# Recurrence output products of a batch: one block of matmuls, or five parts spread over the next two tiles

## The chip, the cores and the metric

The kernel runs on one core of one Trainium2 chip. The metric is the device time of one execution in microseconds (us). The core has five engines with instruction queues of their own: TensorE (PE, matmuls and their weight loads), VectorE (DVE), ScalarE (ACT), GpSimd (POOL) and SyncE (SP, which issues the DMAs). They meet at semaphores.

## What is computed

The reference is one pre-norm layer over x with 4096 rows of 256: an attention block and a small feed-forward block, each added to its input. The attention has 16 heads of 16 channels and two ways to an output, which a gate mixes.

```python
qkv = (x @ Wqkv_w + Wqkv_b).reshape(Bb, Ll, 3, Hh, dd)
attn = jax.nn.softmax(scores + causal_mask, axis=-1)
y_softmax = jnp.einsum('bhij,bhjd->bhid', attn, v)
def step(state, inp):
    q_t, k_t, v_t = inp
    hebbian = v_t[..., :, None] * k_t[..., None, :]
    state = retention * state + Gamma * hebbian
    y_t = jnp.einsum('bhij,bhj->bhi', W_static + state, q_t)
    return (state, y_t)
y = alpha * y_softmax + (1.0 - alpha) * y_stp
```

The second way is a linear recurrence over all 4096 time steps with a 16 x 16 state for each head, whose output at every step is the state (and a static matrix) times the query.

## The kernel before, in words

There are three stages: normalisation and projections (up to about 230 us), attention and recurrence side by side (up to about 1950 us), and a last stage with gate, output projection and feed-forward. The change lies in the middle one.

*Softmax attention.* Four heads make a group, and there are four groups. Queries stand in 8 chunks of 512, taken in the order of `ORDER`, keys in tiles of 128. A group has 144 tiles (`TILES`): one tile is 128 keys against one chunk of queries, for four heads. In a tile TensorE makes four score products `S` (`scores`, L1150, keys by queries, each into a bank of its own), ScalarE takes the exponential of each into `probs` (L1279), and one tile later TensorE makes the values product `V` (`values`, L1166: eight matmul instructions for the four heads, each in a quarter of the columns, into the bank `O_BANK`). The shift in the exponential has to be known before, so the maxima of later chunks are worked out beside this: product `M` (`max_scores`, L1110, queries by keys), of which two side by side go into two banks, and VectorE reduces both with one instruction (L1329). A tile has four `M`, so two maxima. Scores and maximum products use one half of TensorE's rows each (heads stand on two sides), so two that stand next to each other in the order and use different sides run side by side.

*Recurrence.* It runs over 64 units for a group, 16 batches of four (`BATCH`). SyncE loads `v_exp` for each unit (L930), GpSimd multiplies with the keys (L1044), ScalarE scales (L1288), GpSimd sums blocks of four steps (L1054 to L1065), VectorE scans (L1364), and GpSimd weighs the states with the queries (`weigh`, L1077, four instructions, which count the semaphore `weighed`). Then TensorE contracts them: `burst` (L1199) makes static products (L1211), lag products (L1213) and the state products of the four units (L1219), all accumulated in one bank, 128 columns of it. ScalarE evacuates it (`burst_evac`, L1308, to `stp_sb`), and SyncE stores it (L982).

*The order.* Each engine walks the same list of steps, made by `group_steps` (L172), and takes what is its own. In a tile, `TILE_ORDER` (L84) gives the order: S an attention score product, M a maximum product, V values of the tile before and then what `contract` adds, U the evacuations that are due and the recurrence's other steps. `recurrence_steps` (L127) says in which tile they are due: batch B has its period of 9 tiles (8 in the last group); its scan is in tile 9B + 1, its burst after the values of tile 9B + 6, and the evacuation at U of the following tile, behind that tile's first score. `lag` steps and the transposes of shifts and outputs (`turn`, at a tile's end) stand in the same list.

*The banks.* PSUM has eight: three (`S_BANKS`) go round in rotation (`next_bank`) among scores, bursts, lags and turns, four are for maxima, one for the values. `emptied_before` (L258) gives each user of a bank what it has to wait for: the exponential, evacuation or turn that emptied it.

Of the kernel before, what the change touches and what calls it, by code (L numbers as in the profile page):

```python
# [63 lines left out]
STEP4 = 4  # L64
BLOCKS = CH // STEP4
LAGS = STEP4 - 1
# [14 lines left out]
S_BANKS = 3  # L81
M_BANKS = 4
O_BANK = S_BANKS + M_BANKS
TILE_ORDER = "SUMMSSMMSV"  # L84
RING = 2 * BATCH
PAIR = CH // 2
UNITS_PER_CHUNK = 7
# [84 lines left out]
def group_steps(last):  # L172


    steps, turns, pending, evacuations = [], [], [], []
    todo = [(0,) + x for x in ITEMS[AHEAD:]] + ([] if last else [(1,) + x for x in ITEMS[:AHEAD]])
    used = 0
    recurrence = recurrence_steps(last)

    def next_bank():  # L180
        nonlocal used
        used += 1
        return (used - 1) % S_BANKS

    def maximum():
        d, s, n = todo.pop(0)
        steps.append(("max", d, s, n))
        if n == MAXES[s] - 1:
            steps.append(("fold", d, s))
            turns.append([SHIFT_LEAD, "shift_turn", "shift_split", d, s])  # L190

    def turn():
        if turns and turns[0][0] > 0:
            turns[0][0] -= 1
        elif turns:
            _, into, out_of, d, s = turns.pop(0)
            bank = next_bank()
            steps.extend([(into, d, s, bank), (out_of, d, s, bank)])

    def values():  # L200
        s, kt = pending.pop(0)
        steps.append(("values", 0, s, kt))
        if kt == KEY_TILES[s] - 1:
            steps.append(("out_evac", 0, s))
            turns.append([OUT_LEAD, "out_turn", "out_norm", 0, s])

    def recurrent(t, kinds):
        for step in recurrence.get(t, ()):
            if step[0] in kinds:
                steps.append(step)  # L210

    def contract(t):
        for step in recurrence.get(t, ()):
            if step[0] in ("burst", "lag"):
                bank = next_bank()
                steps.append(step + (bank,))
                evacuations.append((step[0] + "_evac",) + step[1:] + (bank,))

    for s in range(NCH):
        for kt in range(KEY_TILES[s]):  # L220
            t = TILE_AT[s] + kt
            for d, names in ((0, LATER), (1, [] if last else EARLY)):
                for name in names:
                    n = t - LOADS[name][2] - d * TILES
                    if 0 <= n < transfers(name):
                        steps.append(("load", d, name, n))
            h = 0
            for kind in TILE_ORDER:
                if kind == "S":
                    steps.append(("scores", 0, s, kt, h, next_bank()))  # L230
                    h += 1
                elif kind == "M" and todo:
                    maximum()
                elif kind == "V":
                    if pending:
                        values()
                    contract(t)
                elif kind == "U":
                    steps.extend(evacuations)
                    evacuations.clear()  # L240
                    recurrent(t, ("kq_load", "v_load", "scan", "scale"))
            turn()
            pending.append((s, kt))
    assert not todo and max(recurrence) < TILES
    values()
    steps.extend(evacuations)
    while turns:
        turns[0][0] = 0
        turn()
    return steps  # L250
# [7 lines left out]
def emptied_before(steps, tail):  # L258


    found, before = {}, dict(tail)
    counts = {"exp": 0, "turn": 0, "burst": 0, "lag": 0}
    for x in steps:
        if x[0] == "scores":
            kind, bank, fills, empties = "exp", x[5], True, True
        elif x[0] in ("shift_turn", "out_turn"):
            kind, bank, fills, empties = "turn", x[3], True, True
        elif x[0] in ("burst", "burst_evac"):
            kind, bank, fills, empties = "burst", x[3], x[0] == "burst", x[0] == "burst_evac"
        elif x[0] in ("lag", "lag_evac"):  # L270
            kind, bank, fills, empties = "lag", x[4], x[0] == "lag", x[0] == "lag_evac"
        else:
            continue
        if fills:
            found[x[:{"exp": 5, "lag": 4}.get(kind, 3)]] = before.get(bank)
        if empties:
            before[bank] = (kind, counts[kind])
            counts[kind] += 1
    return found, {bank: (kind, n - counts[kind]) for bank, (kind, n) in before.items()}
# [12 lines left out]
def preln_attention_ffn_kernel(nc, x, wqkv, bqkv, out_w, out_b, w_static, lam, gamma, gate_w1,  # L292
                               gate_b1, gate_w2, gate_b2, ffn_wt, ffn_b, out):
    ctx = ExitStack()
    with ctx:
# [563 lines left out]
        with att:  # L859
# [22 lines left out]
            with nc.Block() as block:  # L882
# [226 lines left out]
                def _(pe):  # L1109
# [86 lines left out]
                            at += width  # L1196
                        mm.then_inc(lag_ready, 1)

                    def burst(g, B, bank):  # L1199
                        b, q = B // SWEEP_BATCHES, B % SWEEP_BATCHES  # L1200
                        half = b % HALF

                        def rows(e):
                            return PS[e * VW:(e + 1) * VW, bank, 0:BLOCKS]

                        if q == 0:
                            pe.wait_ge(lag_summed, g * (2 * N_SWEEPS) + 2 * b + 2)
                        pe.wait_ge(weighed, g * UNITS + BATCH * B + BATCH + 2 * BATCH)
                        now = q_rows[:, b % 2, 1:1 + CH].rearrange("p (c e) -> p e c", e=STEP4)
                        for e in range(STEP4):  # L1210
                            pe.matmul(rows(e), static_j[:, half, q * VW:(q + 1) * VW], now[:, e], start=True, stop=False)  # L1211
                        for e in range(LAGS):
                            pe.matmul(rows(e), ident[:, q * VW:(q + 1) * VW], lags[:, b % 2, e * BLOCKS:(e + 1) * BLOCKS],  # L1213
                                      start=False, stop=False)
                        for k in range(BATCH):
                            own = state[:, B % 2, k]
                            for e in range(STEP4):
                                first = 1 + e if e < LAGS else 0
                                mm = pe.matmul(rows(e), sum_e[:, half, q * BATCH + k, e, :],  # L1219
                                               own[:, 1 + e:1 + e + STEP4 * (BLOCKS - 1) + 1:STEP4],  # L1220
                                               start=False, stop=(k == BATCH - 1))
                        mm.then_inc(burst_done, 1)

                    def walk(group, steps, emptied, turns_before):
                        for step in steps:
                            kind, g, s = step[0], group + step[1], step[2]
                            if kind == "max":
                                max_scores(g, s, step[3])
                            elif kind == "scores":
                                wait_emptied(group, emptied[step[:5]], turns_before)  # L1230
                                scores(g, s, step[3], step[4], step[5])
                            elif kind == "values":
                                values(g, s, step[3])
                            elif kind == "burst":
                                wait_emptied(group, emptied[step[:3]], turns_before)
                                burst(g, s, step[3])
                            elif kind == "lag":
                                if emptied[step[:4]]:
                                    wait_emptied(group, emptied[step[:4]], turns_before)
                                lag(g, s, step[3], step[4])  # L1240
                            elif kind == "shift_turn":

                                pe.wait_ge(folded, g * NCH + s + 1)
                                if emptied[step[:3]]:
                                    wait_emptied(group, emptied[step[:3]], turns_before)
                                pe.transpose(PS[0:GH * TPC, step[3], 0:P], neg_max[:, s % 2, :], ident[:, :])\
                                    .then_inc(shift_turned, 1)
                            elif kind == "out_turn":

                                pe.wait_ge(out_evacuated, g * NCH + s + 2)  # L1250
                                wait_emptied(group, emptied[step[:3]], turns_before)
                                for j in range(TPC):
                                    mm = pe.transpose(PS[:, step[3], j * P:(j + 1) * P], o_t[:, s % 2, j * P:(j + 1) * P],
                                                      ident[:, :])
                                mm.then_inc(out_turned, 1)
# [499 lines left out]
```

## Time and profile before

| what | us |
|---|---|
| time, median of 3 runs | 2127.93 |
| lowest and highest of them | 2119.26, 2133.13 |
| profiled execution, its own time | 2120.3 |
| its span, first to last instruction | 2118.6 |

The span leaves 1.7 us of the execution's own time outside. The rows further down are of this execution. "Idle" in brackets is the time that an engine stood still just before the instruction, with the one that released it behind the arrow. Rows of a timeline are merged: x2 means two instructions, and the time beside the start is what they cover together.

### The profile page before, as it was taken

The numbers are of one execution on the slowest core, as the hardware profiler recorded it, in microseconds if no ns is written. First come the engines' busy times: TensorE is split into PE (matmuls) and PEld (weight loads), VectorE is DVE, ScalarE is ACT, GpSimd is POOL, SyncE is SP. The second block draws the span as 40 slices with busy tenths as digits, with TensorE's granted clock in tenths as the row PEclk, the third lists the DMA queues.
The fourth block names the chain that finished last, engine by engine and source line by source line (L and its number), as shares of the span: only waits on it lengthen the run. The fifth ranks groups of instructions, "written<-read, shape, count | busy, mean of one in ns | idle before, by whom it ended". The sixth has DMA issues, their size and how long they took to land. (4 is left out here: it accounts for less than half of the span.)

```text
span 2118.6 us, 47123 instructions
## 1 busy us (share of the span) xinstructions
PE 1800.1 (85%) x15280; PEld 718.8 (34%) x15280; DVE 1558.5 (74%) x1712; ACT 1368.7 (65%) x2853; POOL 1153.0 (54%) x1130
## 2 busy tenths in 40 slices
PE   5995589999999899999989999999899998986743
PEld 3552133333334333333343323333433233322632
DVE  5334988888788778887878888878888788601767
ACT  2441067777776777777767777777677777875221
POOL 3102246565666566666666666666567757630535
PEclk9996589999999999999999999999999999998865
DMA  4778041232122412321224124112242121102601
GB/s 127 194 192 198 12 89 59 67 78 64 50 67 66 95 57 69 79 66 50 66 63 99 56 65 94 55 47 79 59 107 67 46 75 45 51 8 57 190 0 79
DMA packets 144582, 163.60 MB, mean 77 GB/s; under 512 B 63440, under 2 KB 91088, under 8 KB 144336
## 3 DMA queue, kind: packets, MB, share of 16 engines
q1 hardware_dynamic: 141952, 158.74, 27.9%
q8 instruction: 131, 2.15, 0.4%
q10 hardware_dynamic: 2384, 1.77, 0.3%
q14 instruction: 115, 0.94, 0.2%
HBM read 122.00 MB, written 38.01 MB: 76 GB/s over the span
## 5 line engine op out<-in xcount | busy, mean ns | idle before, releaser
L1329 DVE TENSOR_REDUCE pmax<-PS 128x2 f32<-128x1024 f32 (+3 forms) x1152 | 1252.5, 1131 | 268.1 <-PE PS L1126 218.2
L1279 ACT ACTIVATE probs<-PS 128x512 f32<-128x512 f32 (+3 forms) x2304 | 1149.5, 566 | 441.9 <-PE PS L1160 336.5
L1160 PE MATMUL PS<-Q_st,K_st 50*128 50x512 f16 (+3 forms) x1408 | 419.0, 360 | 65.9 <-ACT stp_sb L1308 24.7
L1126 PE MATMUL PS<-K_st,Q_st 48*128 48x512 f16 (+3 forms) x1408 | 349.2, 360 | 23.4 <-DVE pmax L1329 22.1
L1181 PE MATMUL PS<-probs,V_g 128*17 128x512 f32 (+3 forms) x2816 | 339.2, 554 | 0.0
L1044 POOL TENSOR_TENSOR v_exp<-v_exp,k_rows 128x512 f32<-128x512 f32 x256 | 321.1, 1287 | 16.7 <-DMA v_exp<-qkv_t 13.7
L1160 PE MATMUL PS<-Q_st,K_first 50*128 50x512 f16 (+3 forms) x896 | 281.6, 382 | 38.8 <-ACT stp_sb L1308 15.2
L1126 PE MATMUL PS<-K_first,Q_st 48*128 48x512 f16 (+2 forms) x896 | 240.6, 413 | 54.3 <-DVE pmax L1329 40.8
L1077 POOL TENSOR_TENSOR state<-ends,q_rows 128x516 f32<-128x516 f32 x256 | 276.1, 1111 | 0.0
L1072 POOL COPY carry<-ends 128x4 f32<-128x4 f32 x64 | 12.1, 189 | 457.1 <-DVE ends L1364 457.1
L1160 PEld LDWEIGHTS PS<-Q_st,K_st 50*128 50x128 f16 x1408 | 113.6, 93 | 418.4 <-ACT probs L1279 296.2
L1054 POOL TENSOR_TENSOR pairs<-pairs,v_exp 128x512 f32<-128x512 f32 x128 | 165.7, 1295 | 135.2 <-ACT pairs L1288 135.2
L1181 PE MATMUL PS<-probs,V_first 128*17 128x512 f32 (+3 forms) x1792 | 230.2, 586 | 0.0
L1160 PEld LDWEIGHTS PS<-Q_st,K_first 50*128 50x128 f16 x896 | 73.3, 94 | 289.1 <-ACT probs L1279 203.3
L1219 PE MATMUL PS<-state,sum_e 128*32 128x128 f32 x2048 | 142.9, 408 | 0.0
L1288 ACT ACTIVATE pairs<-v_exp,decay 128x256 f32<-128x256 f32 x256 | 132.5, 519 | 0.3
L1135 PE MATMUL PS<-mask_kq_sides,ident_sides 64*128 64x128 bf16 x1024 | 124.7, 215 | 0.0
L1126 PEld LDWEIGHTS PS<-K_st,Q_st 48*128 48x128 f16 x1408 | 84.4, 93 | 75.4 <-DVE pmax L1329 68.5
L1135 PE MATMUL PS<-mask_qk_sides,ident_sides 64*128 64x128 bf16 x1024 | 104.9, 222 | 0.0
L1219 PEld LDWEIGHTS PS<-state,sum_e 128*32 128x32 f32 x2048 | 90.7, 123 | 20.0
L1364 DVE TENSOR_TENSOR_SCAN ends<-decay_x,sums 128x516 f32<-128x516 f32 x64 | 79.3, 1240 | 22.4 <-POOL sums L1065 22.4
L621 PE MATMUL PS<-xn_t,wqkv_sb 128*128 128x512 f32 x192 | 94.2, 652 | 1.8 <-ACT xn_t L678 1.8
(163 smaller groups left out, 1569.8 us busy)
## 6 DMA issues: line engine op xcount, KB each, us to landing
v_exp<-qkv_t SPq DMA_DIRECT2D x256, 256.0 KB
qkv_t<-proj SPq DMA_DIRECT2D x24, 512.0 KB, 3.7
qk_parts<-parts SPq DMA_DIRECT2D x16, 512.0 KB, 5.3
Q_st<-qk_parts SPq DMA_DIRECT2D x192, 32.0 KB, 3.4
v_rows<-vaug SPq DMA_DIRECT2D x32, 136.0 KB, 6.1
xin<-x SPq DMA_DIRECT2D x8, 512.0 KB, 6.0
k_rows<-qkv_t SPq DMA_DIRECT2D x16, 256.0 KB, 4.7
q_rows<-qkv_t SPq DMA_DIRECT2D x16, 256.0 KB, 6.8
```

The costliest lines, as they stand in the source:

```text
L621: mm = pe.matmul(PS[:, 2 + u % 4, :], w, xn_t[:, par, c, :], start=(c == 0), stop=(c == HALF - 1))
L1044: pool.tensor_tensor(v_exp[:, n % RING], v_exp[:, n % RING], k_rows[:, b % 2], ALU.mult)\
L1054: pool.tensor_tensor(pairs[:, B % 2, k:k + 2], pairs[:, B % 2, k:k + 2], v_exp[:, slot:slot + 2, 1:CH:2], ALU.add).then_inc(pair_made, 1)
L1077: pool.tensor_tensor(state[:, B % 2, k].rearrange("p (c e) -> p c e", e=STEP4), ends[:, B % 2, k].unsqueeze(2).broadcast_to([P, BLOCKS + 1 ...
L1126: mm = pe.matmul(PS[:, bank, 0:width], Q_st[rows, c, pair, j * P:(j + 1) * P], keys[rows, pair, blk * CH:blk * CH + width], start=True, st ...
L1135: mm = pe.matmul(bank, ident_sides[rows, half, :], mask[rows, half, :], start=False, stop=(half == 1))
L1160: mm = pe.matmul(PS[:, bank, 0:CH - r * P], keys[rows, pair, kt * P:(kt + 1) * P], Q_st[rows, c, pair, r * P:CH], start=True, stop=(kt < T ...
L1181: mm = pe.matmul(PS[h * VW:h * VW + VN, O_BANK, r * P:CH], v[:, kt, h * VN:(h + 1) * VN], probs[:, tile % P_SLOTS, h, 0:CH - r * P], start ...
L1219: mm = pe.matmul(rows(e), sum_e[:, half, q * BATCH + k, e, :], own[:, 1 + e:1 + e + STEP4 * (BLOCKS - 1) + 1:STEP4], start=False, stop=(k ...
L1279: act.activation(probs[:, tile % P_SLOTS, h, 0:CH - r * P], PS[:, step[5], 0:CH - r * P], ACT.Exp, scale=SCORE_SCALE).then_inc(exp_done, 1)
L1288: act.activation(pairs[:, B % 2, s % BATCH, :], v_exp[:, s % RING, 0:CH:2], ACT.Identity, scale=decay[:, 0, col:col + 1]).then_inc(u_scale ...
L1329: dve.tensor_reduce(pmax[:, s % 2, pair * TPC + j:GH * TPC:PAIRS * TPC, blk], PS[:, bank:bank + SIDES, 0:width], AX.X, ALU.max).then_inc(m ...
```

## The change

`TILE_ORDER` gets three places `R` in a tile: after the first pair of maximum products, after the second and third score, and after the second pair of maximum products. A burst is no longer issued after the values of its tile. There its bank is only taken (`held`) and five parts are queued (`BURST_PARTS`): part 0 has the static and lag products, parts 1 to 4 the state products of one unit each. Each `R` issues one part if there is one: three in the next tile, two in the one after. While the bank is held, `next_bank` skips it, so that two banks go round. The evacuation is due at the U after the last part, and the bank is given back there, before the second score of that tile is given its bank. The wait for `weighed` is made for each unit instead of once for the batch. With no part queued, the order of a tile is as before.

```diff
--- before.py
+++ after.py
@@ -81,7 +81,8 @@
 S_BANKS = 3
 M_BANKS = 4
 O_BANK = S_BANKS + M_BANKS
-TILE_ORDER = "SUMMSSMMSV"
+TILE_ORDER = "SUMMRSSRMMRSV"
+BURST_PARTS = 1 + BATCH
 RING = 2 * BATCH
 PAIR = CH // 2
 UNITS_PER_CHUNK = 7
@@ -175,11 +176,14 @@
     steps, turns, pending, evacuations = [], [], [], []
     todo = [(0,) + x for x in ITEMS[AHEAD:]] + ([] if last else [(1,) + x for x in ITEMS[:AHEAD]])
     used = 0
+    held, parts = [], []
     recurrence = recurrence_steps(last)
 
     def next_bank():
         nonlocal used
         used += 1
+        while (used - 1) % S_BANKS in held:
+            used += 1
         return (used - 1) % S_BANKS
 
     def maximum():
@@ -211,10 +215,20 @@
 
     def contract(t):
         for step in recurrence.get(t, ()):
-            if step[0] in ("burst", "lag"):
+            if step[0] == "lag":
                 bank = next_bank()
                 steps.append(step + (bank,))
                 evacuations.append((step[0] + "_evac",) + step[1:] + (bank,))
+            elif step[0] == "burst":
+                held.append(next_bank())
+                parts.extend([step + (held[0], part) for part in range(BURST_PARTS)])
+
+    def burst_part():
+        if parts:
+            step = parts.pop(0)
+            steps.append(step)
+            if not parts:
+                evacuations.append(("burst_evac",) + step[1:4])
 
     for s in range(NCH):
         for kt in range(KEY_TILES[s]):
@@ -235,8 +249,12 @@
                     if pending:
                         values()
                     contract(t)
+                elif kind == "R":
+                    burst_part()
                 elif kind == "U":
                     steps.extend(evacuations)
+                    if "burst_evac" in [x[0] for x in evacuations]:
+                        held.clear()
                     evacuations.clear()
                     recurrent(t, ("kq_load", "v_load", "scan", "scale"))
             turn()
@@ -266,7 +284,7 @@
         elif x[0] in ("shift_turn", "out_turn"):
             kind, bank, fills, empties = "turn", x[3], True, True
         elif x[0] in ("burst", "burst_evac"):
-            kind, bank, fills, empties = "burst", x[3], x[0] == "burst", x[0] == "burst_evac"
+            kind, bank, fills, empties = "burst", x[3], x[0] == "burst" and x[4] == 0, x[0] == "burst_evac"
         elif x[0] in ("lag", "lag_evac"):
             kind, bank, fills, empties = "lag", x[4], x[0] == "lag", x[0] == "lag_evac"
         else:
@@ -1196,30 +1214,33 @@
                             at += width
                         mm.then_inc(lag_ready, 1)
 
-                    def burst(g, B, bank):
+                    def burst(g, B, bank, part):
                         b, q = B // SWEEP_BATCHES, B % SWEEP_BATCHES
                         half = b % HALF
 
                         def rows(e):
                             return PS[e * VW:(e + 1) * VW, bank, 0:BLOCKS]
 
+                        if part > 0:
+                            k = part - 1
+
+                            pe.wait_ge(weighed, g * UNITS + BATCH * B + k + 1 + 2 * BATCH)
+                            own = state[:, B % 2, k]
+                            for e in range(STEP4):
+                                mm = pe.matmul(rows(e), sum_e[:, half, q * BATCH + k, e, :],
+                                               own[:, 1 + e:1 + e + STEP4 * (BLOCKS - 1) + 1:STEP4],
+                                               start=False, stop=(k == BATCH - 1))
+                            if k == BATCH - 1:
+                                mm.then_inc(burst_done, 1)
+                            return
                         if q == 0:
                             pe.wait_ge(lag_summed, g * (2 * N_SWEEPS) + 2 * b + 2)
-                        pe.wait_ge(weighed, g * UNITS + BATCH * B + BATCH + 2 * BATCH)
                         now = q_rows[:, b % 2, 1:1 + CH].rearrange("p (c e) -> p e c", e=STEP4)
                         for e in range(STEP4):
                             pe.matmul(rows(e), static_j[:, half, q * VW:(q + 1) * VW], now[:, e], start=True, stop=False)
                         for e in range(LAGS):
                             pe.matmul(rows(e), ident[:, q * VW:(q + 1) * VW], lags[:, b % 2, e * BLOCKS:(e + 1) * BLOCKS],
                                       start=False, stop=False)
-                        for k in range(BATCH):
-                            own = state[:, B % 2, k]
-                            for e in range(STEP4):
-                                first = 1 + e if e < LAGS else 0
-                                mm = pe.matmul(rows(e), sum_e[:, half, q * BATCH + k, e, :],
-                                               own[:, 1 + e:1 + e + STEP4 * (BLOCKS - 1) + 1:STEP4],
-                                               start=False, stop=(k == BATCH - 1))
-                        mm.then_inc(burst_done, 1)
 
                     def walk(group, steps, emptied, turns_before):
                         for step in steps:
@@ -1232,8 +1253,9 @@
                             elif kind == "values":
                                 values(g, s, step[3])
                             elif kind == "burst":
-                                wait_emptied(group, emptied[step[:3]], turns_before)
-                                burst(g, s, step[3])
+                                if step[4] == 0:
+                                    wait_emptied(group, emptied[step[:3]], turns_before)
+                                burst(g, s, step[3], step[4])
                             elif kind == "lag":
                                 if emptied[step[:4]]:
                                     wait_emptied(group, emptied[step[:4]], turns_before)
```

## Rows read from the trace of the kernel before

**Rows 1.** Page: the span, busy time by engine (share of the span, instructions)
```profile
span 2118.6 us, 47123 instructions
...
PE 1800.1 (85%) x15280; PEld 718.8 (34%) x15280; DVE 1558.5 (74%) x1712; ACT 1368.7 (65%) x2853; POOL 1153.0 (54%) x1130
```

**Rows 2.** Page, costliest groups: busy us, mean ns | idle us before, what ended it
```profile
L1329 DVE TENSOR_REDUCE pmax<-PS 128x2 f32<-128x1024 f32 (+3 forms) x1152 | 1252.5, 1131 | 268.1 <-PE PS L1126 218.2
```

**Rows 3.** Timeline of VectorE around a burst: start us, us, operation [idle before <-releaser]
```profile
911.74 7.12 DVE L1329 TENSOR_REDUCE pmax<-PS 128x2 f32<-128x1024 f32 x6 [0.55 <-PE PS L1126]
921.37 2.26 DVE L1329 TENSOR_REDUCE pmax<-PS 128x2 f32<-128x1024 f32 x2 [2.52 <-PE PS L1126]
924.27 4.74 DVE L1329 TENSOR_REDUCE pmax<-PS 128x2 f32<-128x1024 f32 x4 [0.64 <-PE PS L1126]
```

**Rows 4.** Timeline of TensorE, from an ordinary tile through a burst to tile 8
```profile
915.85 0.39 PE L1160 MATMUL PS<-Q_st,K_st 50*128 50x512 f16 x1
915.85 0.60 PE L1126 MATMUL PS<-K_st,Q_st 48*128 48x512 f16 x2
916.08 0.59 PE L1160 MATMUL PS<-Q_st,K_st 50*128 50x512 f16 x2
916.53 0.39 PE L1126 MATMUL PS<-K_st,Q_st 48*128 48x512 f16 x2
916.93 0.39 PE L1160 MATMUL PS<-Q_st,K_st 50*128 50x512 f16 x1
917.24 1.05 PE L1181 MATMUL PS<-probs,V_g 128*17 128x512 f32 x8
918.11 0.64 PE L1211 MATMUL PS<-q_rows,static_j 128*32 128x128 f32 x8
...
918.79 2.01 PE L1219 MATMUL PS<-state,sum_e 128*32 128x128 f32 x31
920.73 0.39 PE L1160 MATMUL PS<-Q_st,K_st 50*128 50x512 f16 x1
...
921.97 0.39 PE L1160 MATMUL PS<-Q_st,K_st 50*128 50x512 f16 x1 [0.64 <-ACT stp_sb L1308]
...
922.65 1.05 PE L1181 MATMUL PS<-probs,V_g 128*17 128x512 f32 x8
923.63 0.39 PE L1160 MATMUL PS<-Q_st,K_st 50*128 50x512 f16 x1
```

**Rows 5.** Source line L1219, matmuls: duration ns min/median/max
```profile
L1219 PE MATMUL PS<-state,sum_e x2048: 385/408/429, 292.5 to 1902.2; 128*32 128x128 f32 x187
```

**Rows 6.** Timeline of ScalarE, exponentials and the evacuation of the burst
```profile
921.15 0.60 ACT L1279 ACTIVATE probs<-PS 128x512 f32<-128x512 f32 x1 [2.81 <-PE PS L1160]
921.65 0.27 ACT L1308 ACTIVATE stp_sb<-PS 128x128 f32<-128x128 f32 x1
...
916.27 0.60 ACT L1279 ACTIVATE probs<-PS 128x512 f32<-128x512 f32 x1 [0.31 <-PE PS L1160]
```

**Rows 7.** Timelines of VectorE, then TensorE, around the scan of another batch
```profile
483.84 1.22 DVE L1364 TENSOR_TENSOR_SCAN ends<-decay_x,sums 128x516 f32<-128x516 f32 x1
484.98 6.37 DVE L1329 TENSOR_REDUCE pmax<-PS 128x2 f32<-128x1024 f32 x6
...
484.69 1.05 PE L1181 MATMUL PS<-probs,V_g 128*17 128x512 f32 x8
...
487.36 0.39 PE L1126 MATMUL PS<-K_st,Q_st 48*128 48x512 f16 x2 [0.53 <-DVE pmax L1329]
...
487.90 1.05 PE L1181 MATMUL PS<-probs,V_g 128*17 128x512 f32 x8
```

**Rows 8.** Timelines of SyncE (queue), then GpSimd, after the burst of rows 4
```profile
923.53 3.31 SPq L930 DMA_DIRECT2D v_exp<-qkv_t  x4
...
930.46 4.31 POOL L1077 TENSOR_TENSOR state<-ends,q_rows 128x516 f32<-128x516 f32 x4
...
945.62 4.95 POOL L1044 TENSOR_TENSOR v_exp<-v_exp,k_rows 128x512 f32<-128x512 f32 x4
```

## The prediction

> **What bounds the kernel now.** I read the page first. TensorE has the most busy time, 85% of the span, VectorE 74% [rows 1]; but the busy time of overlapping matmuls is no proof of a bound, so the question is who waits in the attention stage. The costliest group is VectorE's maxima (L1329): 268 us of idle time stand before them, 218 of it ended by a score matmul of TensorE [rows 2]. The VectorE timeline around one burst shows where that idle time lies: maxima run without a gap from 911.74 for 7.12 us, then come 2.52 us of idle time, two maxima, and 0.64 us more [rows 3]. That is 3.16 us for a burst, and 64 bursts make 202 of the 268 us. The TensorE timeline of the same place [rows 4] shows what VectorE waits for. I call the tile whose end holds the burst tile 6 (as in the first period of nine) and those after it 7, 8, 9.
>
> An ordinary tile takes 2.375 us: VectorE does six maxima, three tiles, in 7.12 us [rows 3]. TensorE isn't full in it. Scores S0 and the first maximum product start together at 915.85, one on each half of the rows; the next two scores start 0.23 and 0.44 later; the second pair of maximum products 0.68 after the start; S3 at 1.08; values at 1.39, and they take 0.98 until the next score (922.65 to 923.63) [rows 4]. S3 reuses S0's bank and starts when S0's exponential is out: that begins 0.42 after S0 and lasts 0.60 [rows 6]. Without waits the eight products, two side by side, want four steps of 0.22, so TensorE needs 0.88 + 0.98 = 1.87 us and has 0.5 us of waiting in a tile, which an inserted part could use.
>
> **What a burst costs.** Values begin at 917.24, the burst at 918.11, the next score at 920.73 [rows 4]. Values to score takes 0.98 otherwise, so the burst adds 3.49 - 0.98 = 2.50 us. In tile 7, S2 wants the burst's bank and is held until 921.97, 1.24 us after S0, by the evacuation, which stands behind S0's exponential on ScalarE [rows 4, 6]. That tile takes 2.90 (920.73 to 923.63), 0.52 over an ordinary one. Together 3.02 us.
>
> **The change part by part.** The matmuls stay the same in number and shape. Part 0 has static and lag products: 918.11 to the first of the 31 state products at 918.79, 0.68 us. The state products start within 2.01 us, less the 0.41 of the last one [rows 4, 5]: the last starts at 920.39. A record of 0.41 against the 0.17 by which a 512-column score's record (0.39) exceeds the 0.22 step leaves 0.23 of streaming, so the array is free at 920.62, and the four state parts take 1.84 / 4 = 0.46 each.
>
> *Changing between the kinds.* Score and maximum products use half the rows and all columns, burst and values products all rows and a quarter of the columns. From rows 4: S3 to values takes 0.31 where one product streams for about 0.22, so entering costs 0.10. The array is free at 920.62 and the score starts at 920.73, so leaving costs 0.10 (0.11 without rounding). Values to burst takes 0.87 against 0.98 to a score: no such gap between two products of one kind. Now the burst stands behind values and is entered free; after the change each of five parts is entered from scores or maxima and left to them. By my reading the rule in the Trainium skill, TensorEngine Tiling (Array Packing), Key Properties, that a change of the tiling mode drains TensorE, is this effect; the trace agrees, with 0.10 and 0.11 us here; without it the sum would be the first rival's.
>
> *Tile 7* is then, from S0: S0 beside the first maximum product 0; the second alone 0.22 (S1, its neighbour now, stands behind the part); part 0 at 0.53, ends 1.21; S1 beside S2 1.31; part 1 at 1.62 to 2.08; maxima 2.18; part 2 at 2.49 to 2.95; S3 3.05; values 3.36; tile 8 at 4.35. *Tile 8*: second product 0.22; part 3 at 0.53 to 0.99; S1, S2 1.09; part 4 at 1.40 to 1.86; maxima 1.96; S3 2.18; values 2.49; tile 9 at 3.48. Together 7.83, where burst, tile 7's and tile 8's ordinary lengths take 2.50 + 2 x 2.375 = 7.25 now. So +0.58 us a burst, x 64 = +37 us. The 0.5 us of waiting in each tile is used, but ten changes at about 0.1 and two lost pairings at 0.22 eat more.
>
> *Two score banks.* A bank is free 0.42 + 0.60 + 0.05 = 1.07 after its score (915.85 to 916.93 is such a pair) [rows 4, 6]. In the times above S2 comes 1.31 and 1.09 after S0, and S3 1.74 and 1.09 after S1: all just past it. So nothing, at most 0.1 a tile. VectorE's maxima, at most 1.23 each, have time inside 4.35 and 3.48. Behind the waiting score stand maxima products, but those pairs of banks are then free anyway.
>
> *The evacuation* moves to tile 9. Counting the rotation through (burst bank X, then X+1, X+2 alternately until the next step U), S2 of tile 9 takes X again, with the evacuation behind S0's exponential as now: the same 0.52 us, moved by two tiles. Nothing is gained.
>
> *The scan.* The scan of the next batch now goes alone into a full VectorE in tile 10: 1.22 us, maxima follow without a gap, and TensorE's second pair waits 0.53 for them; values come 3.21 after the last instead of 2.375 [rows 7], a delay of 0.84. With the change tile 10 follows the 2.90 us tile directly. A pair is ready 0.64 after its tile's start (920.73 to 921.37 [rows 3, 4]). In tile 9 the second pair, issued behind the held S2 at 1.33, is ready at 1.97 and reduced by 3.20; the first pair of tile 10 is ready at 2.90 + 0.64 = 3.54. So 0.34 of the scan lies in a gap. The scan ends at 4.42 and two queued maxima, 2.26 together as at 921.37 [rows 3], at 6.68; tile 11 starts at 2.90 + 2.38 = 5.28 and can issue its second pair at about 6.77, 1.5 after its start, where now it is 1.69 (484.69 + 0.98 to 487.36 [rows 7]). So 0.2 comes back: 48 bursts of the first three groups, -10 us (between 0 and -0.34 x 48 = -16). In the last group the period is 8, and scan and evacuation share a tile: the last maximum of tile 8 ends at 0.13, the scan at 1.37, two queued maxima at 3.63, where the next pair is ready at 3.54; so 0.8 comes back, 15 times: -12 us (between 0 and -13).
>
> *Turns.* About 25 transposes fall at the end of tile 7 or 8 and use one of two banks; VectorE frees it before S1, which stands behind a part. +2 us (0 to +5).
>
> *Queues.* SP issues the burst's store and, right behind, the four v_exp loads of a later batch; they go at 923.53 and are wanted at 945.62 [rows 8]. Two tiles later, about 6 us, leaves 16. GpSimd needs the burst only two batches on. So this costs nothing; with less than 6 us between the two, GpSimd, VectorE's scan and then the bursts would be late by what is missing.
>
> **Sum.** 37 - 10 - 12 + 2 = +17 us on the profiled execution's own 2120.3 (the span of 2118.6 and 1.7 around it, which stay), so 2137. That execution is 7.6 us under the median 2127.9 of the runs; on it I forecast 2145, +0.8%. A measurement of this kernel can tell about 1% from no change.
>
> **Rivals.**
> A. *Changes are free* (weights of the next kind load while the last stream runs). Then tile 7 is 0.43 + 0.68 + 0.22 + 0.46 + 0.22 + 0.46 + 0.22 + 0.98 = 3.67; in tile 8 S2 waits for its bank (1.07), and 1.07 + 0.22 + 0.46 + 0.42 + 0.22 + 0.98 = 3.37; 7.04 in all: -0.21 x 64 = -13; the scan's -22 and +2 stay: -33, so 2095. For it: TensorE's weight loads do overlap in scores of different halves. Against it: the 0.31 and the 0.34 from the last burst product to the score [rows 4, 5]. It decides from a cost under 0.05 a change.
> B. *Slower clearly: each change drains to the end of the record.* Score records exceed their streaming by 0.17, not 0.10. If a part's first product waits for that, ten changes cost 0.07 more: 0.7 x 64 = +45, 2190. For it: nowhere in the trace is a part entered from two products that stream side by side. Against: rows 4 show values 0.31 after S3. It decides at 0.15 a change, where the sum passes +2%.
> C. *The scan gives all back.* If VectorE were the bound everywhere, its idle time at tile 9 would take in the whole 0.84 of each scan: 63 x -0.84 = -53, with +37 and +2 that is -14, 2114. Against it: the gap before the scan is 0.34 long.
> D. *The change does not do what it says*, as its parts could all wait for the last state product. GpSimd's four state products of the next batch start at 930.46 and are through after 4.31 us [rows 8], some three tiles ahead of their burst, so the waits find their counts reached; its chance is below 0.02 and inside the others'.
>
> **How the numbers follow.** Forecast 0.50, with 2145 +- 15 from its own bounds (scan 0 to -29, turns, bank waits of 0.1 x 128 = 13): two fifths of it lie above +1%. A 0.17, B 0.20, C 0.13. Faster by over 1% (below 2107): most of A, 0.15. Slower by over 1% (above 2149): 0.20 of the forecast's and B's 0.20, 0.40. Within 1%: 0.45. The range goes from A, 2095, to near B, 2180.
>
> **What would show it.** State products in groups of eight in tiles 7 and 8, 0.46 us each, with 0.31 from the score before and 0.10 after the array is free: if the gaps are under 0.05, A. Tiles 7, 8, 9 of 4.35, 3.48, 2.90. VectorE's one gap of 2.5 us replaced by four of 0.3 to 0.7. S2 still held by the evacuation in tile 9, 64 times. VectorE's idle time before L1329 rising by some 17 us. A tile 7 under 4.0 us would make the forecast wrong.

## The result, and the profile after

The changed kernel takes 2150.0 us (median of 4 runs, 2148.3 to 2156.2), the kernel before 2125.1 on the same measurement; the ratio is 1.012, 95% interval 1.0079 to 1.0161. It is slower by 25 us. The profiled execution took 2149.57 us.

The page of the changed kernel, its span, busy times and costliest group, against [rows 1, 2]. The line numbers have moved: L1351 is the maxima, L1144 the maximum products, L1178 the scores, L1199 values, L1230 the state products of a part, L1240 and L1242 static and lag products, L1330 the burst's evacuation.

```profile
span 2147.7 us, 47255 instructions
...
PE 1854.4 (86%) x15280; PEld 665.6 (31%) x15280; DVE 1568.6 (73%) x1712; ACT 1389.9 (65%) x2853; POOL 1152.3 (54%) x1130
...
L1351 DVE TENSOR_REDUCE pmax<-PS 128x2 f32<-128x1024 f32 (+3 forms) x1152 | 1262.7, 1131 | 289.9 <-PE PS L1144 214.7
```

The same matmuls (x15280), and TensorE is "busy" for 54 us more: I read this so: busy time is what the records cover together, and a record lasts 0.39 us where the next could start after 0.22, so products that overlap less fill more time with the same work. The matmul records agree: their durations add up to 6379 us before and 6367 after, nearly the same, while the time that they cover together rises. VectorE's idle time before its maxima rose from 268 to 290 us; the change meant to fill that gap has made it larger.

TensorE's timeline from tile 7 to the start of tile 9 (start us, us), to be held against [rows 4]. The first score of a tile is the L1178 line at 907.65, 912.07 and 915.55.

```profile
907.65 0.39 PE L1178 MATMUL PS<-Q_st,K_st 50*128 50x512 f16 x1
907.66 0.60 PE L1144 MATMUL PS<-K_st,Q_st 48*128 48x512 f16 x2
908.19 0.65 PE L1240 MATMUL PS<-q_rows,static_j 128*32 128x128 f32 x8
908.63 0.42 PE L1242 MATMUL PS<-lags,ident 128*32 128x128 f32 x6
908.98 0.39 PE L1178 MATMUL PS<-Q_st,K_st 50*128 50x512 f16 x2
909.30 0.64 PE L1230 MATMUL PS<-state,sum_e 128*32 128x128 f32 x8
909.87 0.39 PE L1144 MATMUL PS<-K_st,Q_st 48*128 48x512 f16 x2
910.19 0.64 PE L1230 MATMUL PS<-state,sum_e 128*32 128x128 f32 x8
910.77 0.39 PE L1178 MATMUL PS<-Q_st,K_st 50*128 50x512 f16 x1
911.08 1.05 PE L1199 MATMUL PS<-probs,V_g 128*17 128x512 f32 x8
912.07 0.39 PE L1178 MATMUL PS<-Q_st,K_st 50*128 50x512 f16 x1
...
912.60 0.64 PE L1230 MATMUL PS<-state,sum_e 128*32 128x128 f32 x8
913.17 0.39 PE L1178 MATMUL PS<-Q_st,K_st 50*128 50x512 f16 x2
913.49 0.64 PE L1230 MATMUL PS<-state,sum_e 128*32 128x128 f32 x8
...
915.55 0.39 PE L1178 MATMUL PS<-Q_st,K_st 50*128 50x512 f16 x1
...
916.80 0.39 PE L1178 MATMUL PS<-Q_st,K_st 50*128 50x512 f16 x1 [0.64 <-ACT stp_sb L1330]
...
918.40 0.39 PE L1178 MATMUL PS<-Q_st,K_st 50*128 50x512 f16 x1
```

Read the distances between lines. Here tile 7 takes 4.42 us, tile 8 3.48, tile 9 2.85. From one kind to the other: scores at 908.98 to the part at 909.30 is 0.32, where two scores would stand 0.22 apart; the part to the maxima at 909.87 is 0.57, where the four parts took 0.46 each in one block. So from one pair of products to the next, with a part between, it takes 0.89 us, where the pair needs 0.22 and the part 0.46: 0.21 is the price of the two changes. The score at 916.80 is held by the evacuation, 1.25 us after its tile's first score, as at 921.97 in [rows 4].

VectorE's timeline of the same stretch, against [rows 3].

```profile
910.33 1.23 DVE L1351 TENSOR_REDUCE pmax<-PS 128x2 f32<-128x1024 f32 x1 [0.81 <-PE PS L1144]
912.71 1.23 DVE L1351 TENSOR_REDUCE pmax<-PS 128x2 f32<-128x1024 f32 x1 [1.15 <-PE PS L1144]
914.49 0.43 DVE L1351 TENSOR_REDUCE pmax<-PS 128x2 f32<-128x256 f32 x1 [0.56 <-PE PS L1153]
916.19 2.47 DVE L1351 TENSOR_REDUCE pmax<-PS 128x2 f32<-128x1024 f32 x2 [1.27 <-PE PS L1144]
918.58 1.22 DVE L1386 TENSOR_TENSOR_SCAN ends<-decay_x,sums 128x516 f32<-128x516 f32 x1
919.72 6.37 DVE L1351 TENSOR_REDUCE pmax<-PS 128x2 f32<-128x1024 f32 x6
```

One gap of 2.52 and one of 0.64 have become four, 3.79 us together (the 256-wide maximum ends early and lengthens one by 0.8). What VectorE got earlier in tile 7 it paid for in the next gaps: it never works faster than TensorE delivers pairs.

With the start of the first score of each of the 576 tiles in both traces, the whole adds up. From tile 6 to tile 9 the changed kernel takes 39.8 us more over the 64 batches (0.68 in the median batch). In the tiles where the scan's delay falls (tile 11 in the first three groups, tile 10 in the last) it takes 14.1 less: 7.7 in 48 tiles and 6.3 in 15. All other tiles of the stage take 1.4 more. That is +27.1. A further 4.6 us lie before the first tile (its first score is at 273.78 before and 278.38 after), in code that is the same; other executions start that tile anywhere from 272.1 to 280.0. The last stage, also the same code, is 2.6 us shorter, so the spans differ by 29.1.

The granted clock bears on such sums. In short stretches of the attention stage it is 0.50 (1.2 GHz) where it is 1.00 otherwise (2.4 GHz), and a score's record lasts about 0.63 us instead of 0.39. One covers the first 8 us from 691.7 in the trace before, behind 3 us in which TensorE stood still; the other traces have more or fewer of them (22 us at 0.50 from 1879 where the evacuation goes first in the changed kernel). Without the 17 tiles that hold such a record in one of the two traces, the changed kernel takes 31.2 us more in the stage. So a difference of two single traces is uncertain by several us, and the medians of the runs decide about times.

### The profile page after: what moved, and what is told of

Same layout as the page of the kernel before. It is cut to its first block and busy times, and to the rows that moved or that the text cites. A ratio compares the mean times of both kernels' runs of the same rounds, so it can differ in the third digit from the quotient of the medians.

```text
span 2147.7 us, 47255 instructions
## 1 busy us (share of the span) xinstructions
PE 1854.4 (86%) x15280; PEld 665.6 (31%) x15280; DVE 1568.6 (73%) x1712; ACT 1389.9 (65%) x2853; POOL 1152.3 (54%) x1130
## 5 line engine op out<-in xcount | busy, mean ns | idle before, releaser
L1351 DVE TENSOR_REDUCE pmax<-PS 128x2 f32<-128x1024 f32 (+3 forms) x1152 | 1262.7, 1131 | 289.9 <-PE PS L1144 214.7
L1301 ACT ACTIVATE probs<-PS 128x512 f32<-128x512 f32 (+3 forms) x2304 | 1168.3, 564 | 448.0 <-PE PS L1178 335.9
L1178 PE MATMUL PS<-Q_st,K_st 50*128 50x512 f16 (+3 forms) x1408 | 418.8, 363 | 57.8 <-ACT stp_sb L1330 24.3
L1144 PE MATMUL PS<-K_st,Q_st 48*128 48x512 f16 (+3 forms) x1408 | 350.0, 362 | 10.7 <-DVE pmax L1351 10.0
L1199 PE MATMUL PS<-probs,V_g 128*17 128x512 f32 (+3 forms) x2816 | 341.6, 558 | 0.0
L1178 PE MATMUL PS<-Q_st,K_first 50*128 50x512 f16 (+3 forms) x896 | 277.8, 379 | 36.8 <-ACT stp_sb L1330 15.8
L1144 PE MATMUL PS<-K_first,Q_st 48*128 48x512 f16 (+2 forms) x896 | 235.2, 410 | 52.8 <-DVE pmax L1351 38.0
L1178 PEld LDWEIGHTS PS<-Q_st,K_st 50*128 50x128 f16 x1408 | 112.2, 93 | 444.0 <-ACT probs L1301 336.6
L1199 PE MATMUL PS<-probs,V_first 128*17 128x512 f32 (+3 forms) x1792 | 228.7, 583 | 0.0
L1178 PEld LDWEIGHTS PS<-Q_st,K_first 50*128 50x128 f16 x896 | 71.8, 93 | 304.0 <-ACT probs L1301 228.2
L1230 PE MATMUL PS<-state,sum_e 128*32 128x128 f32 x2048 | 163.4, 400 | 0.0
L1144 PEld LDWEIGHTS PS<-K_st,Q_st 48*128 48x128 f16 x1408 | 82.2, 93 | 75.4 <-DVE pmax L1351 67.4
L1153 PE MATMUL PS<-mask_qk_sides,ident_sides 64*128 64x128 bf16 x1024 | 98.8, 222 | 0.0
L1144 PEld LDWEIGHTS PS<-K_first,Q_st 48*128 48x128 f16 x896 | 55.5, 95 | 112.1 <-DVE pmax L1351 89.7
```

Of the source, the lines that this page charges most:

```text
L1144: mm = pe.matmul(PS[:, bank, 0:width], Q_st[rows, c, pair, j * P:(j + 1) * P], keys[rows, pair, blk * CH:blk * CH + width], start=True, st ...
L1153: mm = pe.matmul(bank, ident_sides[rows, half, :], mask[rows, half, :], start=False, stop=(half == 1))
L1178: mm = pe.matmul(PS[:, bank, 0:CH - r * P], keys[rows, pair, kt * P:(kt + 1) * P], Q_st[rows, c, pair, r * P:CH], start=True, stop=(kt < T ...
L1199: mm = pe.matmul(PS[h * VW:h * VW + VN, O_BANK, r * P:CH], v[:, kt, h * VN:(h + 1) * VN], probs[:, tile % P_SLOTS, h, 0:CH - r * P], start ...
L1301: act.activation(probs[:, tile % P_SLOTS, h, 0:CH - r * P], PS[:, step[5], 0:CH - r * P], ACT.Exp, scale=SCORE_SCALE).then_inc(exp_done, 1)
L1351: dve.tensor_reduce(pmax[:, s % 2, pair * TPC + j:GH * TPC:PAIRS * TPC, blk], PS[:, bank:bank + SIDES, 0:width], AX.X, ALU.max).then_inc(m ...
```

## The experiments

Each run was measured with the kernel before on the same chip. Medians of the kernel before were 2126.8 us for the experiments with two parts together, with either evacuation edit and with the block two tiles later, and 2123.6 for the other four. Ratios are to these.

**Two parts together.**

```diff
-TILE_ORDER = "SUMMRSSRMMRSV"
+TILE_ORDER = "SUMMRSSRRMMSV"
```

> The changed kernel, order SUMMRSSRRMMSV: part 2 stands directly behind part 1, the rest as it is. Theory K (each change between score or maximum products and burst products costs TensorE about 0.2 us, in and out): one pair of changes fewer in tile 7, which goes from 4.42 to 4.15-4.20 us; 0.2 to 0.25 x 64 = 13 to 16 us less than the changed kernel's 2150, so 2135. Rival H (what costs is the bank held over two tiles, that is waits of scores on exponentials): no change, 2150. Rival D (VectorE has to be fed early, so a later second pair costs): slower than 2150.

Measured: 2138.0 us, ratio to before 1.0051 (1.0020 to 1.0082). TensorE's timeline of tile 7 in this kernel:

```profile
901.02 0.39 PE L1178 MATMUL PS<-Q_st,K_st 50*128 50x512 f16 x1
...
902.35 0.39 PE L1178 MATMUL PS<-Q_st,K_st 50*128 50x512 f16 x2
902.66 1.10 PE L1230 MATMUL PS<-state,sum_e 128*32 128x128 f32 x16
903.70 0.39 PE L1144 MATMUL PS<-K_st,Q_st 48*128 48x512 f16 x2
...
905.22 0.39 PE L1178 MATMUL PS<-Q_st,K_st 50*128 50x512 f16 x1
```

The tile takes 4.20 us instead of 4.42. Sixteen state products take 1.04 from their start to the maxima, where two parts apart take 2 x 0.57. So H falls, since the held bank is the same here and 12 us go all the same, and D falls, since the time does not rise though VectorE gets its second pair behind both parts.

**The last part before the values.**

```diff
-TILE_ORDER = "SUMMRSSRMMRSV"
+TILE_ORDER = "SUMMRSSRMMSRV"
```

> The changed kernel, order SUMMRSSRMMSRV: part 2 stands behind the fourth score, directly before the values product, which is of its own kind. Theory K (a change between the kinds costs about 0.1 us each way, none between burst and values products): leaving part 2 becomes free and one entry is saved as the fourth score's own change is taken over by it, so tile 7 goes from 4.42 to about 4.20, the same 13 us as with two parts together, though the parts stand apart: 2137. Rival (the saving there was that of the sequencer or of a semaphore wait when parts follow each other): no change, 2150.

Measured: 2135.5 us, ratio 1.0040 (1.0008 to 1.0072). TensorE's timeline of tile 7:

```profile
900.52 0.39 PE L1178 MATMUL PS<-Q_st,K_st 50*128 50x512 f16 x1
...
902.16 0.65 PE L1230 MATMUL PS<-state,sum_e 128*32 128x128 f32 x8
902.74 0.39 PE L1144 MATMUL PS<-K_st,Q_st 48*128 48x512 f16 x2
902.97 0.38 PE L1178 MATMUL PS<-Q_st,K_st 50*128 50x512 f16 x1
903.28 0.64 PE L1230 MATMUL PS<-state,sum_e 128*32 128x128 f32 x8
903.72 1.06 PE L1199 MATMUL PS<-probs,V_g 128*17 128x512 f32 x8
904.71 0.39 PE L1178 MATMUL PS<-Q_st,K_st 50*128 50x512 f16 x1
```

The tile takes 4.19 us. Here the parts stay apart, with their own waits on `weighed`, and 0.22 goes as before: the maxima go over into the score with no change between (0.23), and the values begin 0.44 after their part, where maxima begin 0.57 or 0.58 after one. So it is the change between the kinds, and not the parts' following each other, that has the price.

The kinds differ in more than their tiles: scores and maxima are fp16 and use half of the rows, parts and values are fp32 and use all of them. Two lines of the kernel before settle this much, the values of a tile that `lag` products follow:

```profile
754.23 1.05 PE L1181 MATMUL PS<-probs,V_first 128*17 128x512 f32 x8
755.22 0.91 PE L1194 MATMUL PS<-kq,lag_sum 128*128 128x384 f32 x2
```

Both are fp32 and use all the rows, but the second uses all the columns. It begins 0.99 after the values (0.98 in the median of 15 such places), as a score does, and not 0.87, as a burst does. So the price comes with another share of the columns alone, and needs no change of the number type. What TensorE waits for in it (the end of the last stream, or the weights of the next kind) no run here separates.

**The evacuation ahead of the first score, in the changed kernel.** In both versions of this edit the list of evacuations is emitted ahead of the tile's steps and not at U.

```diff
+            released = "burst_evac" in [x[0] for x in evacuations]
+            steps.extend(evacuations)
+            evacuations.clear()
             h = 0
             for kind in TILE_ORDER:
...
                 elif kind == "U":
-                    steps.extend(evacuations)
-                    if "burst_evac" in [x[0] for x in evacuations]:
+                    if released:
                         held.clear()
-                    evacuations.clear()
```

> The changed kernel with the evacuations (of bursts and of lags) ahead of the tile's first score instead of behind it, the bank still given back at U. Tile 9 goes from 2.85 to 2.38 us, 0.47 x 64 = -30 us. But if the 2.85 us tile is what lets the scan of tile 10 run in a gap, as the trace says (tile 11 is 2.85 instead of 3.21), 0.36 x 48 = +17 and about +6 in the last group come back: -7 us, 2143. If the scan's gain has another cause, 2120.

Measured: 2116.3 us, ratio 0.9951 (0.9919 to 0.9983), 27 us under the first number and 4 under the second. That it is near the second does not mean that the scan's gain had another cause: the trace says that both reasons of the first number were right and a third was missing. Tile 9 goes from 2.85 to 2.38, and tile 11 back from 2.85 to 3.21, so the scan had lived off that gap. But the two tiles behind the `lag` products, 3.91 and 3.17 us long in the third batch of a group, go to 3.37 and 2.44. Over the 15 such places this is 1.04 to 1.49 us each, 18 us in all, which the sum above left out. The scan gives back less than the 23 us that were expected, about 10 in the tiles at full clock.

**The same edit in the kernel before.**

```diff
+            steps.extend(evacuations)
+            evacuations.clear()
             h = 0
             for kind in TILE_ORDER:
...
                 elif kind == "U":
-                    steps.extend(evacuations)
-                    evacuations.clear()
```

> The kernel before with the evacuations ahead of the tile's first score. ScalarE then evacuates the burst between its end and the end of the first score, while it has nothing else: tile 7 goes from 2.90 to 2.38-2.43 us, 0.47 x 64 = -30, and the 32 lag evacuations give a few us more: 2125 - 33 = 2092. Tiles 8 to 11 unchanged, since the scan stands two tiles away. If the third score was held by something else than the order on ScalarE: 2125.

Measured: 2083.2 us, ratio 0.9788 (0.9728 to 0.9847). ScalarE and TensorE behind a burst:

```profile
905.95 2.00 PE L1219 MATMUL PS<-state,sum_e 128*32 128x128 f32 x31
...
907.89 0.39 PE L1160 MATMUL PS<-Q_st,K_st 50*128 50x512 f16 x1
...
908.38 0.28 ACT L1308 ACTIVATE stp_sb<-PS 128x128 f32<-128x128 f32 x1 [2.87 <-PE PS L1219]
908.55 2.06 ACT L1279 ACTIVATE probs<-PS 128x512 f32<-128x512 f32 x4
...
908.71 0.39 PE L1160 MATMUL PS<-Q_st,K_st 50*128 50x512 f16 x1 [0.22 <-ACT stp_sb L1308]
...
910.50 0.39 PE L1160 MATMUL PS<-Q_st,K_st 50*128 50x512 f16 x1
```

The held score starts 0.82 us after the first one instead of 1.24, and the tile takes 2.61 here (2.38 in most batches, where it was 2.84). The evacuation begins later than I had thought, 0.49 after the first score's start, but the first exponential is delayed by only 0.24. It helps by 43 us, 10 more than expected; the tiles behind the `lag` products again give 18, where I had put 3.

**The block two tiles later, no parts.**

```diff
-SCAN_AT, SCALE_AT, BURST_AT, KQ_AT, LAG_AT = 1, 1, 6, 2, 3
+SCAN_AT, SCALE_AT, BURST_AT, KQ_AT, LAG_AT = 1, 1, 8, 2, 3
```

> The kernel before with BURST_AT 8 instead of 6: the burst stays one block behind the values, two tiles later, so that its evacuation is in tile 9 and the 2.85 us tile stands directly before the scan, as in the changed kernel, but with no parts and no bank held. If the scan falls into the gap: tile 11 from 3.21 to 2.85, 0.36 x 48 = -17, last group 0.5 x 15 = -8: 2125 - 25 = 2100. If the place of the burst doesn't matter: 2125. The difference between the changed kernel and this one is then the price of the parts, 50 us or 0.78 a burst.

Measured: 2117.3 us, ratio 0.9965 (0.9931 to 0.9998); 9 us of the 25, and no more than just clear of the noise. In an ordinary batch it is as expected, tile 11 at 2.85 instead of 3.21. But such batches are few: the scan's tiles give 13 us back in all, about as in the changed kernel, not 25. And in five batches of each of the first three groups the block now meets other things (masks at the end of a chunk, turns): its tile takes 5.3 to 5.5 us instead of 4.9, and six or seven batches of such a group lose 0.15 to 0.7. So an ordinary tile is too good a price for the place of a block. The changed kernel takes 33 us more than this one, 0.51 a burst: that is the price of the parts with the bank held, where I had expected 50.

**Two banks, and nothing else.** The changed kernel without R in the order; all parts are issued behind the values of tile 8, but the bank is held from the end of tile 6.

```diff
-TILE_ORDER = "SUMMRSSRMMRSV"
+TILE_ORDER = "SUMMSSMMSV"
...
+                due[:] = [t + 2]
                 parts.extend([step + (held[0], part) for part in range(BURST_PARTS)])
...
+                    if parts and due[0] == t:
+                        while parts:
+                            burst_part()
                     contract(t)
-                elif kind == "R":
-                    burst_part()
```

> The changed kernel without R in the order: the bank is taken at the end of tile 6 and held, but all five parts are issued as one block behind the values of tile 8. Against the kernel before with the block there (2117) it differs by the two banks alone. Theory: in a tile without parts the third score then waits 1.07 us for the first one's exponential, and the second pair of maximum products stands behind it: tiles 7 and 8 take 2.7 to 2.8 instead of 2.38, +0.35 x 2 x 64 = +45, 2160. In the changed kernel this wait is covered by the parts themselves. Rival (two banks cost nothing here either): 2117.

Measured: 2182.4 us, ratio 1.0257 (1.0195 to 1.0320), 65 us over the same block without the hold (two measurements, 2182.4 and 2117.3; the ratios to the kernel before say 68 or so). TensorE in tile 7:

```profile
918.21 0.39 PE L1180 MATMUL PS<-Q_st,K_st 50*128 50x512 f16 x1
...
919.28 0.39 PE L1180 MATMUL PS<-Q_st,K_st 50*128 50x512 f16 x1 [0.47 <-ACT probs L1303]
...
921.08 0.39 PE L1180 MATMUL PS<-Q_st,K_st 50*128 50x512 f16 x1
```

The third score starts 1.07 us after the first, released by the exponential, and the tile takes 2.87: 0.49 more than 2.38, x 2 x 64 = 63. So two banks do have a price, larger than I put it, in a tile with nothing in between. In the changed kernel the third score comes 1.33 and 1.10 us after the first, past the 1.07, and pays none of it.

**The scan in the block's gap.** In the kernel before, the block goes as far back as it can:

```diff
-        add(t + BURST_AT, "burst", 0, B)
+        add(min(t + period, TILES - 1), "burst", 0, B)
```

> The kernel before with the burst of a batch three tiles later (period tiles after the start of its period, at the latest in the group's last tile), still one block. Then the scan of the next batch is what VectorE finds when the block begins, in the 2.5 us gap. If the scan's price is VectorE's time in a full stretch, its 0.84 (tile 11 at 3.21 instead of 2.38) goes in most of 48 batches and 0.65 in 15: about -45, 2080. If TensorE is held in that stretch by something else: 2126.

Measured: 2102.2 us, ratio 0.9874 (0.9822 to 0.9927), a gain of 21, half of what was expected. Tile 11's wait is gone in ordinary batches (2.38 for 3.21), but as in the block two tiles later, the batches whose block has moved next to masks and turns give part of it back, and in 28 of the 48 the scan had cost under 0.5 before.

**Both edits.** The block ahead of the scan and the evacuation first.

> Both edits that helped, on the kernel before: evacuations ahead of the first score (2083 by itself) and the burst one tile before the next scan. They touch different waits (a held score bank, VectorE's queue), so they should add: 2083 - 45 = 2038. But with the evacuation ahead, the tile behind the block is 2.38 instead of 2.85 us, and VectorE, which has spent 1.22 of its gap on the scan, may be late in it: then 0.3 x 64 less of gain, 2055.

Measured: 2057.3 us, ratio 0.9670 (0.9617 to 0.9723), 66 us under the kernel before and 93 under the changed one; the fastest of all. The two gains (43 and 21) add to 64. That the time is so near the 2055 of the second expectation is luck: the scan's gain was put at 45 and is 21. VectorE around a block:

```profile
898.09 4.73 DVE L1329 TENSOR_REDUCE pmax<-PS 128x2 f32<-128x1024 f32 x4 [0.29 <-PE PS L1126]
902.74 1.22 DVE L1364 TENSOR_TENSOR_SCAN ends<-decay_x,sums 128x516 f32<-128x516 f32 x1
905.36 4.74 DVE L1329 TENSOR_REDUCE pmax<-PS 128x2 f32<-128x1024 f32 x4 [1.39 <-PE PS L1126]
```

The scan takes 1.22 of the gap of [rows 3], 1.39 is left, and nothing is late behind it: the tile after the block takes 2.38 with both edits. The second part of what I expected, a loss of 0.3, is not there.

## Why the prediction was right

The forecast was 2145 and the time is 2150; the sign, the mechanism and the size of the main term hold. As a difference it was +17 us, and it is +25: the forecast stood on a median of 2127.9, and the kernel before gave 2125.1 beside the result, which hides 3 of the 8 us.

*Tile by tile.* Tile 7 was forecast at 4.35, tile 8 at 3.48, tile 9 at 2.90. The batch shown took 4.42, 3.48 and 2.85, but its tile 8 is one of the shortest, as its second pair of maxima is 128 wide. Without masks and turns the medians are 4.41, 3.52 and 2.84. The median batch loses 0.68, not 0.58, and the term of +37 us (with +2 for the turns) is 39.8. Batches with a turn in tile 7 or 8 lose 0.81 in the median, 0.13 more, fifteen times: the +2 holds. VectorE's gaps were forecast at 0.3 to 0.7 each and are 0.56 to 1.27, 3.79 together, and its idle time before the maxima rose by 22 us, not 17.

*The changes between the kinds.* Forecast at 0.10 each way; 0.22 for a pair in two experiments that each take one pair away, 12 and 14.5 us in all (13.7 and 13.0 if each kernel is held against the kernel before of its own measurement). Rival A (changes are free) falls by that, and rival B (0.17 for an entry) too. Five parts have ten changes, 5 x 0.21 x 64 = 67 us, where the whole loss is 25: by this estimate the parts would have gained without them. No run takes all ten away. The two lost pairings were seen (the second maximum product stands alone in tiles 7 and 8) but not tried apart.

*Two banks.* That they cost nothing here was right for the reason given, and it was close: without parts in the tile they cost 0.49 us a tile, and the third score of tile 8 clears the exponential by 0.03.

*The evacuation.* Moved by two tiles with its price unchanged, as forecast: 61 waits of scores on L1330 in the profile of after, 40.1 us in sum, against 64 and 39.8 before.

*The scan* is the term that was mis-sized: -10 - 12 forecast; -14.1 measured in its tiles, -7.7 in the first three groups and -6.3 in the last. Not because an ordinary tile 11 gives back too little (0.36, where I took 0.2), but because many batches aren't ordinary: the median of the 48 gives back 0.14. In the last group I let 0.84 of price vanish, where the scan cost only 0.65 in its ordinary batches, and got a median of 0.47 back. 22 forecast against 14.1 is 8 us, most of what lies between the forecast's 17 and the 27.1 measured in the attention stage. Rival C, where the scan gives back all, falls: its whole price came back in no version of this order, only where the scan stands in the block's gap.

*The queues* cost nothing that can be seen: GpSimd's wait for the `v_exp` transfers is 23 us in the after's profile and 14 before, and GpSimd's first instruction behind the scan still waits for VectorE, 472 us in sum (457 before), so it has time to spare.

*Luck.* The profiled execution of after is 29 us above that of before, 27.1 of it in the attention stage, 4.6 ahead of it and -2.6 behind it; the last two are no effect of the change. The range of 2095 to 2180 is wide, and its rival A, a gain, had a chance of 0.17: the forecast of its own mechanism had only 0.50.

## What to carry to other kernels

Idle time inside a tile on TensorE is usable only net of what it costs to get in and out: a piece of 0.46 us between products of another shape cost 0.67 here, and the piece also broke up pairs that ran side by side, so cutting a block in pieces should be priced by the number of changes of shape before it is priced by the gap it fills. A gap that a block of one engine leaves on another is better filled by moving the other engine's lone work into it (the scan), and an evacuation should stand ahead of work that waits for TensorE anyway: those two small edits gave 3.3%, where five parts lost 1.2%. Price such a move over all batches of the schedule, not over the ordinary one.

## What was not expected of the hardware

Two neighbouring products that use the same kind of tiles have no gap (values to burst), and sixteen state products in one part take 1.04 us to the next maxima where two parts of eight take 1.14: the price is that of the change alone, about 0.10 us on the way in and 0.11 to 0.13 on the way out. It is nearly the same after one score or maximum product as after two side by side (0.31 and 0.32 us to the next product). It does not depend on the length of what stands between: from the start of the last state product to the next score or maximum product it is 0.34 us in the median after parts of eight, after sixteen together and after the whole burst of forty-six instructions, and 0.21 to a values product. ScalarE began an evacuation 0.43 us after the end of the last product's record (907.95 to 908.38, in the kernel before with the evacuation first), so an evacuation that stands first still delays the next exponential, by 0.24 us against the 0.42 after its score that it begins in [rows 4, 6].
